# A mixture-of-experts kernel: the single blocks' rows move to GpSimd's queue, their list is read in another order

## The reference

```
x = x + scan_layer(layernorm(x))                 # h @ w_qkva, a = sigmoid(a), y_t = a_t*y_(t-1) + kv_t, q*y
z = layernorm(x)
top_vals, top_idx = top_k(z @ router_w.T, 2);  top_w = softmax(top_vals)
expert(z, e) = (silu(z @ w_gate[e]) * (z @ w_up[e])) @ w_down[e]      # 256 -> 1024 -> 256
x = x + sum over the two chosen experts of top_w * expert(z, e) + shared(z)
```

## Time and profile before

| | us |
|---|---|
| median of 3 executions | 1039.39 (1038.4 to 1040.02) |
| the profiled execution | 1041.65 |
| its span, first to last instruction | 1039.9 |
| TensorE busy | 1007.9 (97%) |
| VectorE busy | 627.5 (60%) |
| ScalarE busy | 523.5 (50%) |
| GpSimd busy | 504.4 (49%) |
| DMA, mean rate | 185 GB/s |

### The profile page before, as it was taken

How to read it: one execution, slowest core, us unless ns; L and a number is a source line. 1 busy time by engine, 2 the same in 40 slices (tenths; PEclk the granted TensorE clock), 3 DMA queues, 4 the chain that set the end, 5 groups by cost and what they waited for, 6 DMA issues and landing times.

```text
span 1039.9 us, 19706 instructions
## 1 busy us (share of the span) xinstructions
PE 1007.9 (97%) x7277; PEld 950.3 (91%) x7277; DVE 627.5 (60%) x1095; ACT 523.5 (50%) x786; POOL 504.4 (49%) x283
## 2 busy tenths in 40 slices
PE   7999999999999796999999999999999999999998
PEld 5788999989999696999999999999999999999997
DVE  7987677787423143555556565656565655547776
ACT  4554433222212255666666666666666666653232
POOL 2236200000010367777877777777877787750000
PEclk9999999999999898999999999999999999999999
DMA  9333300012587727777777777777777777728341
GB/s 314 99 85 81 82 11 21 11 60 78 169 286 262 266 66 262 224 256 233 258 235 256 234 259 229 259 233 261 233 255 239 254 232 256 247 71 242 113 142 40
DMA packets 162029, 192.75 MB, mean 185 GB/s; under 512 B 76089, under 2 KB 147266, under 8 KB 151746
## 3 DMA queue, kind: packets, MB, share of 16 engines
q1 hardware_dynamic: 155248, 173.83, 51.7%
q0 software_dynamic: 6720, 18.36, 5.7%
q10 hardware_dynamic: 18, 0.01, 0.0%
HBM read 165.42 MB, written 26.74 MB: 185 GB/s over the span
## 4 chain that ended last, share of the span: by engine, by line
PE 76%; DVE 9%; DMA 8%; issue 3%; SPq 3%; ACT 1%; POOL 0%; DVEq 0%; POOLq 0%; ACTq 0%
PE ps L1012 46%; PE ps L1027 15%; PE ps L1031 7%; DMA sorted_rows<-x_stage 5%; PE ps L919 3%; DVE y_sb L1200 2%; PE ps L903 1%; PE ps L1053 1%; DMA w_first<-in_L_ffn_w_down_dram 1%; SPq L421 1%; DVE h_early L1516 1%; DVE hT_lo L1160 1%; PE ps L1060 1%; SPq L404 1%; DVE h_lo L1521 1%
## 5 line engine op out<-in xcount | busy, mean ns | idle before, releaser
L1012 PE MATMUL ps<-xs_hi,w_both 128*128 128x256 f32 x3072 | 566.9, 284 | 10.8 <-DVE ps L1516 8.9
L1012 PEld LDWEIGHTS ps<-xs_hi,w_both 128*128 128x128 f32 x3072 | 481.3, 190 | 13.8 <-DVE ps L1516 9.1
L1012 PE MATMUL ps<-xs_lo,w_both 128*128 128x256 f32 x1536 | 436.0, 284 | 0.0
L585 POOL TENSOR_TENSOR w_both<-raw,w_both 128x2048 fp32r<-128x2048 f32 x67 | 318.4, 4752 | 105.3 <-ACT w_both L745 97.0
L1012 PEld LDWEIGHTS ps<-xs_lo,w_both 128*128 128x128 f32 x1536 | 291.8, 190 | 0.1
L1027 PE MATMUL ps<-w_both,h_hi 128*128 128x512 f32 x768 | 273.6, 398 | 0.9 <-DVE h_lo L1521 0.7
L1031 PE MATMUL ps<-w_both,h_lo 128*128 128x256 f32 x768 | 215.5, 281 | 0.0
L784 ACT ACTIVATE silu<-ps 128x512 f32<-128x512 f32 x192 | 114.3, 595 | 199.8 <-PE ps L1012 199.8
L745 ACT ACTIVATE w_both<-raw 128x1024 fp32r<-128x1024 f32 x192 | 192.4, 1051 | 10.6 <-DMA raw<-in_L_ffn_w_up_dram 9.2
L1516 DVE TENSOR_TENSOR ps<-ps,silu 128x512 f32<-128x512 f32 x160 | 111.9, 699 | 133.0 <-ACT silu L784 126.7
L1027 PEld LDWEIGHTS ps<-w_both,h_hi 128*128 128x128 f32 x768 | 144.4, 188 | 35.0 <-DVE h_lo L1521 1.8
(11 more groups left out here) (192 smaller groups left out, 798.7 us busy)
## 6 DMA issues: line engine op xcount, KB each, us to landing
raw<-in_L_ffn_w_up_dram SPq DMA_DIRECT2D x33, 1024.0 KB, 5.3
raw<-in_L_ffn_w_gate_dram SPq DMA_DIRECT2D x33, 1024.0 KB, 8.6
raw<-in_L_ffn_w_down_dram SPq DMA_DIRECT2D x33, 1024.0 KB, 5.5
sorted_rows<-x_stage SPq DMA_DIRECT2D x32, 256.0 KB
x_rows<-sorted_rows SPq DMA_DIRECT2D x128, 64.0 KB, 5.3
got<-expert_rows SPq DMA_DIRECT2D x10, 512.0 KB, 6.1
z_rows<-z_all SPq DMA_DIRECT2D x8, 512.0 KB, 2.9
x_rows<-z_rows SPq DMA_DIRECT2D x64, 64.0 KB, 2.3
```

What stands on the lines that cost most here:

```text
L585: pool.tensor_tensor(w_lo[buf][:, k, :], source[:, k, :], w_hi[buf][:, k, :].bitcast(F32), ALU.subtract).then_inc(wlo_ready[k], 1)
L1012: last = pe.matmul(o, w[:, part, at[kd]:at[kd] + P], xx[:, u, kd, :], start=i == 0, stop=i == len(terms) - 1)
```

## The change

- GpSimd puts and loads the singles' rows, on its own queue and with semaphores of their own (`lone_put`, `lone_ld`), in one row with its gathers and scatters. SP keeps puts and loads of routed blocks and issues the singles' weights one behind the other. `load_lone(0)` now follows `routed`, which comes in slot 7.
- On SP the first routed block's put (`put_x(NS)`) stands before the wait for slot 12 and the load of w_first; before, it stood behind. On GpSimd the two gathers for the first routed blocks stand before scatter 3, and no longer wait for `xT_psum`.
- `lone_in` counts two parts, `lone_down_in` the down part, for which TensorE waits before the down phase. `first_in` becomes three semaphores, and ScalarE waits for the one of the part that it rounds.
- `take_lists` signals `listed` after `idx_x`; the steps for `idx_y` (`take_targets`) follow one pair later. `owners` moves from the end of slot 5 to the end of slot 7. `positions(1)` is cut in two and moves into slots 3 and 4.

```diff
@@ -225,7 +225,10 @@
         lone_in = [sem(f"lone_in{i}") for i in range(NS)]
-        first_in = sem("first_in")
+        lone_down_in = [sem(f"lone_down_in{i}") for i in range(NS)]
+        first_in = [sem(f"first_in{k}") for k in range(3)]
+        lone_put = [sem("lone_put0"), sem("lone_put1")]
+        lone_ld = [sem("lone_ld0"), sem("lone_ld1")]
         consts = sem("consts")
@@ -398,37 +405,30 @@
-            def load_all(i, dst, signal):
+            def load_all(i, dst, signals):
                 sources = rows_of_expert(i)
                 for k in (1, 0, 2):
-                    sp.dma_start(parts_of(dst)[k], sources[k]).then_inc(signal, 16)
+                    sp.dma_start(parts_of(dst)[k], sources[k]).then_inc(signals[k], 16)
...
                 sp.wait_ge(gath[i % 2], signals(i))
-                if i < NS:
-                    sp.dma_start(sorted_dram[i * P:(i + 1) * P], x_stage[:, i % 2, 0, :]).then_inc(x_put[i % 2], 16)
-                else:
-                    sp.dma_start(rows_of(sorted_dram, i - NS + NS // ST), x_stage[:, i % 2, :, :]
-                                 ).then_inc(x_put[i % 2], 16)
+                sp.dma_start(rows_of(sorted_dram, i - NS + NS // ST), x_stage[:, i % 2, :, :]
+                             ).then_inc(x_put[i % 2], 16)
...
                 sp.wait_ge(xT_psum, n + 1)
-                sp.wait_ge(x_put[i % 2], 16 * (i // 2 + 1))
+                sp.wait_ge(x_put[i % 2], 16 * ((i - NS) // 2 + 1))
                 for a in range(NBK):
-                    if i < NS:
-                        sp.dma_start(x_rows[a * BK:(a + 1) * BK, n % 2, 0:P // BK, :], piece_of(sorted_dram, i, P, a)
-                                     ).then_inc(x_ld[n % 2], 16)
-                    else:
-                        sp.dma_start(x_rows[a * BK:(a + 1) * BK, n % 2, :, :],
-                                     piece_of(sorted_dram, i - NS + NS // ST, SLOT, a)).then_inc(x_ld[n % 2], 16)
+                    sp.dma_start(x_rows[a * BK:(a + 1) * BK, n % 2, :, :],
+                                 piece_of(sorted_dram, i - NS + NS // ST, SLOT, a)).then_inc(x_ld[n % 2], 16)
...
                     sp.wait_ge(down_psum, slot_of(i - 3) + 2)
-                load_all(i, w_lone[i], lone_in[i])
+                load_all(i, w_lone[i], (lone_in[i], lone_in[i], lone_down_in[i]))
@@ -447,39 +447,33 @@
             for n in range(4, FIRST_LONE):
                 load_x(n, n, z_dram, n % 2)
-            sp.wait_ge(routed, 1)
             for k in range(3):
                 sp.wait_ge(wlo_ready[k], 1)
+            sp.wait_ge(routed, 1)
             load_lone(0)
             sp.wait_ge(listed, 1)
-            for i in range(2):
-                put_x(i)
-                load_sorted(i)
-            load_lone(1)
-            put_x(2)
-            load_sorted(2)
-            load_lone(2)
+            for i in range(1, 3):
+                load_lone(i)
             load_x(LATE, SA - 1, z_dram, LATE % 2)
             for i in range(3, NS):
                 load_lone(i)
-                put_x(i)
-                load_sorted(i)
+            put_x(NS)
             sp.wait_ge(down_psum, LATE + 2)
             load_all(NS, w_first, first_in)
-            put_x(NS)
             load_sorted(NS)
+            put_x(NS + 1)
             sp.wait_ge(down_psum, slot_of(3) + 2)
             load_expert(1, 1)
-            put_x(NS + 1)
+            sp.wait_ge(xT_psum, slot_of(NS + 1) + 1)
             P0 = 16 * (NS // 2)
             with sp.Fori(0, ROUTED // 2 - 1) as i:
-                load_pair(i * 2 + 1, 1, i * 16 + (P0 + 16))
+                load_pair(i * 2 + 1, 1, i * 16 + 16)
                 put_pair(i * 2 + 2, 0, i * (16 * ST) + (P0 + 32 * ST))
                 load_expert(i * 2 + 2, i * 2 + 3)
-                load_pair(i * 2 + 2, 0, i * 16 + (P0 + 32))
+                load_pair(i * 2 + 2, 0, i * 16 + 32)
                 put_pair(i * 2 + 3, 1, i * (16 * ST) + (P0 + 32 * ST))
                 load_expert(i * 2 + 3, i * 2 + 4)
-            load_pair(ROUTED - 1, 1, P0 + 8 * ROUTED)
+            load_pair(ROUTED - 1, 1, 8 * ROUTED)
             load_w(raw_rows(sw_gate[0], sw_up[0], sw_down[0]), ROUTED + 1)
             for u in range(2):
@@ -604,16 +598,32 @@
-                if i >= NS:
+                if i >= NS + 2:
                     pool.wait_ge(xT_psum, slot_of(i) + 1)
                 if i >= 2:
-                    pool.wait_ge(x_put[i % 2], 16 * (i // 2))
+                    if i - 2 < NS:
+                        pool.wait_ge(lone_put[i % 2], 16 * (i // 2))
+                    else:
+                        pool.wait_ge(x_put[i % 2], 16 * ((i - NS) // 2))
                 for t in range(blocks_of(i)):
...
                         bounds_check=N - 1).then_inc(gath[i % 2], 16)
+            def put_x(i):
+                pool.wait_ge(gath[i % 2], signals(i))
+                pool.dma_start(sorted_dram[i * P:(i + 1) * P], x_stage[:, i % 2, 0, :]).then_inc(lone_put[i % 2], 16)
+            def load_sorted(i):
+                n = slot_of(i)
+                pool.wait_ge(xT_psum, n + 1)
+                pool.wait_ge(lone_put[i % 2], 16 * (i // 2 + 1))
+                for a in range(NBK):
+                    pool.dma_start(x_rows[a * BK:(a + 1) * BK, n % 2, 0:P // BK, :], piece_of(sorted_dram, i, P, a)
+                                   ).then_inc(lone_ld[n % 2], 16)
@@ -628,16 +638,27 @@
             pool.wait_ge(listed, 1)
-            for i in range(4):
+            for i in range(2):
                 gather_x(i)
+                put_x(i)
+            for i in range(2):
+                load_sorted(i)
+            for i in range(2, 4):
+                gather_x(i)
+                put_x(i)
+            load_sorted(2)
+            pool.wait_ge(listed, 2)
             for i in range(2):
                 scatter_y(i)
+                load_sorted(i + 3)
                 gather_x(i + 4)
-            for i in range(2, 4):
-                scatter_y(i)
+                put_x(i + 4)
+            scatter_y(2)
+            load_sorted(5)
             gather_x(NS)
+            gather_x(NS + 1)
+            scatter_y(3)
             split_lo(0, 1, 0, w_first)
-            gather_x(NS + 1)
             scatter_y(4)
             split_lo(2, 1, 0, w_first)
@@ -754,7 +775,7 @@
-                act.wait_ge(first_in, 48)
+                act.wait_ge(first_in[k], 16)
                 round_half(k, 0, w_first, half)
@@ -1041,7 +1062,7 @@
                 pe.wait_ge(xT_psum, n + 3)
-                pe.wait_ge(lone_in[i], 48)
+                pe.wait_ge(lone_in[i], 32)
                 for p in range(PAIRS):
@@ -1053,6 +1074,7 @@
                     last.then_inc(gu_psum, 1)
+                pe.wait_ge(lone_down_in[i], 16)
                 pe.wait_ge(down_free, n + 1)
@@ -1219,9 +1241,10 @@
-            def turn_lone(par, nth):
-                dve.wait_ge(x_ld[par], nth)
+            def turn_lone(i):
+                par = slot_of(i) % 2
+                dve.wait_ge(lone_ld[par], LD * sum(slot_of(k) % 2 == par for k in range(i + 1)))
                 for k in range(KD):
@@ -1464,7 +1490,11 @@
                 step(dve.tensor_scalar(rows_f[:, 1, :], rows_f[:, 1, :], 0.0, None, ALU.max))
-                step(dve.tensor_copy(idx_x[:, :], rows_f[:, 1, :]))
+                dve.tensor_copy(idx_x[:, :], rows_f[:, 1, :]).then_inc(listed, 1)
+            def take_targets():
+                dve.wait_ge(listed, 1)
                 step(dve.tensor_scalar(rows_f[:, 1, :], count_f[:, 0:COLS], float(P), float(TOP * N + P),
@@ -1601,39 +1632,38 @@
                 hot_cols(c + 1)
+            for n in range(3, LISTED):
+                between = {0: lambda n=n: hot_rows(2 * (n - 3)), "down": lambda n=n: lists(n)}
+                if n == 3:
+                    between[2] = lambda: pick(1)
                 if n == 4:
-                    positions(1)
-                if n == 5:
-                    owners()
-            for n in range(3, LISTED):
-                slot(n, n % 2, LD * (n // 2 + 1 + n % 2), shared=n, early=True, skip=0,
-                     between={0: lambda n=n: hot_rows(2 * (n - 3)), "down": lambda n=n: lists(n)})
+                    between[2] = lambda: halves_of(1)
+                slot(n, n % 2, LD * (n // 2 + 1 + n % 2), shared=n, early=True, skip=0, between=between)
             n = LISTED
-            slot(n, n % 2, LD * (n // 2 + 1 + n % 2), shared=n, early=True, skip=0, between={1: take_lists})
+            slot(n, n % 2, LD * (n // 2 + 1 + n % 2), shared=n, early=True, skip=0, between={
+                1: take_lists, 2: take_targets, "down": owners})
```

32 lines of the change are left out of this document (17 added, 15 removed).

## The result

The changed kernel takes 1028.37 us (median of 4, 1028.24 to 1028.54), the kernel before on the same chip 1039.7 us (median of 4, 1038.4 to 1040.96). The ratio is 0.9893 with a 95% interval of 0.9868 to 0.9919, a gain of 11.3 us. The forecast was 1030.7 (8.7 gained), rival A 1028.1. The time lies in the range, and at rival A: the direction and the place were right, the inner terms of the sum were not, as the experiments show.

A forecast was written before the change was run, and what follows sets the result against it. Bound: TensorE, with waits of 8.9, 7.0 and 1.1 us, the 7.0 costing 10.2. Sum 1.1 + 10.2 - 0.4 - 1.0 - 1.2 = 8.7 off the median 1039.39 gives 1030.7; likeliest case 1027.5 to 1032, range up to 1043.

The forecast's parts named there:

- rival A: Slots 9 to 14: GpSimd's plain transfers cost 0.8 or less, or land in 5; 11.3 gained, 1028.1; chance 0.50 with forecast.
- the 8.9 us of slot 17: TensorE's stall in slot 17, starting at GpSimd's gather for the third expert; to move along unchanged, with its slow-clock tail.
- the owners' term: Slots 5 and 6: moving the owners out of slot 5 ends TensorE's 1.1 us wait; 1.1 us gained.
- Single transfers on GpSimd: GpSimd's queue: each plain put or load taken at 1.33 us to issue, like its indirect transfers.
- Landings: GpSimd's row transfers: landing 3.2 us after issue on quiet queues, 6.0 beside weights, 7.4 at the bad end.
- the remaining stall of 1.2: Slot 14: TensorE still waits 1.2 us for w_first's up part in place of 7.0, without slow clock.
- the costs of 0.4 and 1.0 in slots 9 and 11: Late row loads: 3.4 us late in slot 9, costing 0.4; 4.5 late in slot 11, costing 1.0.
- What saves it is the semaphore for each part: Slot 14: w_first is issued no earlier, about 340.1, but ScalarE needs only the up part, landed at 345.0.
- the heart: Moving the singles' rows to GpSimd's queue, taken as the central part: 41 transfers there instead of 12 before w_first.
- one of order on SP, not of bandwidth: Slot 14's 7.0 us stall: w_first asked for 9.8 us late, since slot 15's put sat behind 3 MB of weights on SP.
- the later first weights cost nothing: SP's first single's weights start at about 264 after the owners' move, still in time for slot 9: cost nothing.
- The rule on queues: Skill's rule that another issuing engine saves only issuing time; noted as speaking against the change, trace rows rather against the rule.

The follow-up runs named there:

- gather_first: Changed kernel with GpSimd's gather for the third expert issued ahead of its subtraction of the second expert's gate part: 1020.36 us.
- own_back_hold: Changed kernel with owners and positions(1) back in slots 4 and 5, SP holding the second and third singles' weights until slot 10's put landed: 1030.42 us.
- own_back: Changed kernel with the owners and both halves of positions(1) back in slots 4 and 5: 1035.43 us.
- twice_issued: Changed kernel with each of GpSimd's 24 row loads split in two halves, same bytes: 1032.94 us.
- whole_sem: Changed kernel, but ScalarE waits for all three parts of w_first before rounding the first: 1036.88 us.
- sem_only: Kernel before with only a semaphore for each part of w_first and a separate one for the singles' down part: 1032.93 us.
- queue_only: Changed kernel with owners and positions(1) back in slots 4 and 5 and ScalarE waiting for all parts of w_first: 1042.22 us, ratio 1.0020.
- First_ahead: Kernel before with one edit on SP, w_first's load ahead of slot 15's put and row loads: 1035.43 us.
- own_only: Kernel before with only VectorE's position work moved (owners and targets to slot 7, positions(1) to slots 3 and 4): 1053.68 us.

## Why the prediction was right, and where it was not

**The reading of the bound held.** The stall of 7.0 us was w_first's, it cost 10.2 us with the slow matmuls behind it, and it went; the 1.1 us wait went; the 8.9 us of slot 17 moved along unchanged, and was GpSimd's, as gather_first shows. No new wait came in slots 9 to 15.

**That the median came so close to rival A is partly luck.** A has 1.1 + 10.2 = 11.3 us, and 11.3 is what the medians differ by. But the two traces differ by 13.2, as the owners' term was 1.25 too small and some 0.6 has no part in the change, and the traced execution of the kernel before is 2 us above its median. The forecast took its 10.2 us from this one execution and subtracted them from the median. The differences happen to cancel.

**The owners' term was too small, and its reason incomplete.** 1.1 was forecast, 2.35 came, and own_back_hold, which undoes just this, measures 2.0 to 2.7 (1030.42 against 1028.37 and 1027.70). I took the price from the one wait that the list of waits names. VectorE's lateness also cost three waits of 0.2 to 0.4 us that no row names, and `positions(1)`, whose move I costed at nothing, is one of its causes: it stands for 1.8 us (205.56 to 207.31) in front of slot 5's residual sums and first gate, which come that much later than in the changed kernel.

**Single transfers on GpSimd: 0.55, not 1.33.** I took the indirect ones as the nearest rows, since engine and number of rows were the same, over SP's 0.4. The bound from SP was the near one. 30 x 0.78 = 23 us of GpSimd's time too many.

**Landings: the term was right for puts, too short for gathers.** The two puts beside weights whose landing the trace has took 5.5 and 5.6 us (forecast 6.0), one with nothing beside it 2.1, the gathers beside weights 6.6 to 8.7. Beside heavier traffic puts are no safer: in own_back one took 7.1 (267.40, next to 6 MB asked for from 259.37 on). The row of the puts, from the DMA issues of the changed kernel between 240 and 400 us (what, queue, count, KB, us to landing), is the median of those three:

```profile
sorted_rows<-x_stage POOLq DMA_DIRECT2D x6, 128.0 KB, 5.5
```

From the load at 293.52 to the first expert's gather at 327.76 the changed kernel needs 34.2 us; the sum had 299.9 to 334.2, 34.3. The two errors cancelled there to 0.1. What then made w_first 6.6 us earlier than forecast (333.45, not 340.1) is the start of this stretch: TensorE was 1.7 further ahead than I had it, and the 4.5 us by which slot 11's rows should have been late did not occur, since the issues before them were cheap. So **the remaining stall of 1.2 and the costs of 0.4 and 1.0 in slots 9 and 11** were not paid: 2.6 us, the whole distance from forecast to rival A. In slot 14 it was closer than the sum suggests, since 1.0 us later would have been too late (`twice_issued`). `twice_issued`, with a load at 1.1 us, brings them back: w_first asked for at 339.36 (forecast 340.1), a stall of 1.88 (1.2), no slow clock behind it, small losses of 1.8 us before slot 14.

**"What saves it is the semaphore for each part"** stood in the forecast, and is what whole_sem and sem_only confirm: 8.5 and 7.6 us. But the forecast called the rows on GpSimd's queue the heart. queue_only says that they gain nothing alone. In the whole change they take away the small stalls that sem_only still has in slots 14 and 15, and above all they make the owners' move affordable; beside the semaphore without that move or a wait in its place they cost 2.5 us.

**That the stall was "one of order on SP, not of bandwidth"** was half right. First_ahead asks 9.0 us earlier on the same queue and w_first's end comes 2.9 earlier. The DMA engines were still busy with single 5's weights, which are asked for at 327.55 there, because these had been held up by the puts. In the changed kernel each set of weights goes out as its place comes free (290.96, 299.71, 310.32), and single 5's is in before w_first is asked for.

**That the later first weights cost nothing** was true of the changed kernel only. own_only shows what the same edit costs when rows and weights share a queue, own_back what it costs when the weights come with the first rows on two queues. I looked at whether the weights would be in time, not at what they would hold up.

**The rule on queues.** The trace shows a put beside weights at 5.5 us on GpSimd's queue, against 9.5 on SP's behind single 5's weights, and gathers at 6.6 to 8.7. The clearest case is the put at 303.30: it landed at 308.86, while the gate part that SP had asked for 3.2 us before it landed at 311.46. On SP's own queue the put at 326.90 came in only behind the last of the weights (335.97). The Trainium skill (DMA: Bandwidth & Descriptors, Issuing engines are not separate DMA queues) says that all queues interleave on the same 16 engines and that another issuing engine saves only the issuing. queue_only's 1.0020 agrees with it as a forecast for the sum. The puts speak against reading it as "nothing but the issuing": a short transfer on its own queue did not wait for all that had been asked for before it on the other.

**What stays open.** own_only was run with the owners in slot 7 and the wait for them as it is; whether the owners could stay in slot 5 at no cost to VectorE by standing elsewhere in it was not tried. The executions of the kernel before differ by 2.6 us in the first set (and by 7.7 in the last), those of the changed one by 0.3 to 1.0. The clock goes with it: in the last set the two fastest executions of the kernel before (1036.71 and 1036.77 us) have a mean granted clock of 0.993, the two slowest (1043.45 and 1044.37) 0.989 and 0.988. Why the slow clock lasts longer in one execution than in the next is not known, and there is no trace of a median execution of the kernel before.
